# Attention stage of a two-layer transformer kernel: VectorE keeps the row-maximum stretch for itself, preparation of later batches moves ahead of it, residual add moves to GpSimd

## The chip, the cores and the metric

One NeuronCore of a Trainium2 chip runs the whole kernel. The metric is the device time of one execution in microseconds. The engines are TensorE (PE; its weight loads are listed as PEld), VectorE (DVE), ScalarE (ACT), GpSimd (POOL) and SyncE (SP, which issues transfers).

## The reference

The input `x` has 16 batches of 256 rows by 256 columns; `ctx` has the same shape. Layer 0 is a decayed sum over the rows and a feed-forward block with 4-bit weights. Layer 1 is the attention that this change is about, and then a feed-forward block with block floating point. Cut to the attention:

```python
q = layernorm(x); k = v = ctx                  # 16 heads of 16 columns each
q = q * cos + rotate_half(q) * sin             # k likewise
scores = einsum('bqhd,bkhd->bhqk', q, k) * hd ** -0.5 + slope[h] * (key - query)
attn = softmax(scores)
x = x + tanh(g_xattn[1]) * einsum('bhqk,bkhd->bqhd', attn, v)
```

## The kernel before

Every engine has its own written program, and semaphores tie them together. All 16 batches of `x` stay in SBUF (`xres`). After layer 0 the attention runs over batches 0 to 15, one body (`at_body`) each. Bodies 0, 1, 14 and 15 are written out, and 2 to 13 are a loop of two bodies a turn (`over_batches`).

A body for batch b overlaps three batches. On PE, it first turns (transposes) the operands of batch b+1: eight turns of `a_stack` into `a_ps_t` (`at_turn`, L561), which ACT casts into `stack_t` (L910). Between turns 1 and 2 it turns out the result of batch b-1 (`at_turn_out`, L623). This is called the first part here. In the second part PE makes, for batch b+1, sixteen pairs of matmuls for the row maxima (`at_scores_for_max`, L579, called M0 to M15) and mixes them with the sixteen pairs of the scores of batch b (`at_scores`, L600, S0 to S15) and eight groups of probabilities times values (`at_times_v`, L615, PV0 to PV7). DVE reduces every M to row maxima (`at_row_max`, L1497, R0 to R15). ACT takes the exponential of every S (`at_exponent`, L919, E0 to E15). M, S and their PSUM buffers alternate between the row halves 0 to 63 and 64 to 127 by the parity of their index, and each half has one buffer. So M(m) waits for R(m-2), S(u) waits for E(u-2), and PV(g) waits for E(2g+1). At the end of a body PE turns the maxima (`at_turn_max`, L586), which waits for R15.

The two parts of DVE's body carry, beside the maxima, the preparation of batch b+2: layernorm statistics (`at_qk_a`, L1451 to L1457), the normed q (`at_qk_norm`, L1463 and L1466), the rope sums (`at_rope`, L1475) and a cast of the rounded high half into the stack (`at_high_part`, L1487). They also carry the reciprocal and share of batch b-1 (L1504, L1508) and its gated residual add (L1511). POOL does the rope products (L1148, L1149, L1158, L1159), the reciprocal root (L1153) and the low half of the stack (`at_low_part`, L1141). Before, the k side and the norm stand in DVE's first part, and the rope sum and cast of q stand inside the sixteen maxima, at m = 5 and m = 8.

## Time and profile before

| | |
|---|---|
| median of 3 runs | 862.73 us (856.55 to 863.42) |
| the profiled execution | 860.34 us, span 858.2 us |
| busy share of the span | PE 83%, DVE 83%, ACT 57%, POOL 50% |
| attention bodies 0 to 15 | about 377 to 697 us of the span |
| mean granted PE clock | 0.93; 1.00 in the loop of the attention |

The page gives busy time, the chain of work that ended last and the costliest groups. The timeline gives single instructions, neighbours of one line merged into one row, and what ended the idle time before them.

### The profile page before, as it was taken

What the parts mean: (1) busy time and instruction counts of PE and PEld (TensorE: products, weight loads), DVE (VectorE), ACT (ScalarE), POOL (GpSimd) and SP (SyncE); (2) the same over time, 40 slices, a digit from 0 to 9 for tenths busy, and PEclk for the clock granted to TensorE, in tenths of its full rate; (3) what the DMA queues carried; (4) which work ended last, traced back from release to release, by engine and by line L of the source; (5) the groups of instructions that cost most, each with busy time, mean ns of one, the idle gap of its engine ahead of it and who ended that gap; (6) DMA issues with size and microseconds to landing.
All of it is one profiled execution on the core that took longest, in us unless ns stands there. A gap on an engine that the chain in (4) does not pass through costs nothing.

```text
span 858.2 us, 16571 instructions
## 1 busy us (share of the span) xinstructions
PE 713.5 (83%) x5090; PEld 517.0 (60%) x5090; DVE 708.5 (83%) x1230; ACT 488.0 (57%) x939; POOL 431.1 (50%) x331
## 2 busy tenths in 40 slices
PE   2255999999999998779999999999999775777775
PEld 1255888887888877556565555656565333444444
DVE  6867788998889887868898989898888658888885
ACT  3433545445454342337777777777778674555553
POOL 4524565555655545644444554555443526655553
PEclk8576999999999999879999999999999987888898
DMA  8800000000000000010000000000001000100011
GB/s 279 246 3 0 1 1 1 0 0 0 0 0 1 1 1 1 1 50 2 3 2 2 1 1 1 2 1 1 1 1 50 2 1 1 37 25 24 26 37 50
DMA packets 17719, 18.35 MB, mean 21 GB/s; under 512 B 1670, under 2 KB 16912, under 8 KB 17680
## 3 DMA queue, kind: packets, MB, share of 16 engines
q1 hardware_dynamic: 17084, 17.66, 6.4%
q8 instruction: 21, 0.34, 0.2%
q10 hardware_dynamic: 596, 0.20, 0.1%
q14 instruction: 18, 0.15, 0.1%
HBM read 13.39 MB, written 4.19 MB: 20 GB/s over the span
## 4 chain that ended last, share of the span: by engine, by line
PE 33%; DVE 30%; issue 16%; POOL 9%; ACT 8%; DVEq 1%; DMA 1%; POOLq 1%; ACTq 0%; SPq 0%
PE a_ps_t L561 7%; PE a_ps_m L579 6%; DVE maxima L1497 5%; PE a_ps_pv L615 4%; DVE f_ps_small L1582 4%; PE a_ps_s L600 3%; POOL hs L1110 3%; PE ps_o L522 3%; DVE hup L1324 2%; DVE f_hcode L1598 2%; DVE yup L1293 2%; POOL xres L1090 2%; DVE hscale L1318 2%; ACT hmag L866 1%; PE a_ps_pv L623 1%
## 5 line engine op out<-in xcount | busy, mean ns | idle before, releaser
L1497 DVE TENSOR_REDUCE maxima<-a_ps_m 128x2 f32<-128x512 f32 x256 | 166.3, 687 | 35.4 <-PE a_ps_m L579 34.7
L919 ACT ACTIVATE probs<-a_ps_s 128x512 f32<-128x512 f32 x256 | 149.2, 602 | 42.3 <-PE a_ps_s L600 40.1
L579 PE MATMUL a_ps_m<-stack_t 64*128 64x256 f32 x512 | 107.5, 328 | 19.9 <-DVE maxima L1497 16.7
L579 PEld LDWEIGHTS a_ps_m<-stack_t 64*128 64x128 f32 x512 | 68.3, 188 | 78.7 <-DVE maxima L1497 49.5
L600 PE MATMUL a_ps_s<-stack_t 64*128 64x256 f32 x512 | 100.0, 308 | 3.7 <-ACT probs L919 2.9
L1141 POOL TENSOR_TENSOR stack<-roped,stack 128x512 f32<-128x512 f32 x32 | 42.6, 1333 | 116.8 <-DVE stack L1487 115.3
L491 PE MATMUL ps_gu<-w1h,yth 128*128 128x352 f32 x256 | 88.6, 346 | 13.2 <-DVE h L1311 13.2
L522 PE MATMUL ps_o<-w2t,hqt 128*128 128x256 f32 (+1 forms) x384 | 97.9, 390 | 0.2 <-ACT hqt L851 0.2
L615 PE MATMUL a_ps_pv<-probs,v_aug 128*32 128x256 f32 x1024 | 83.0, 396 | 2.9 <-ACT probs L919 2.5
L910 ACT CAST stack_t<-a_ps_t 128x512 fp32r<-128x512 f32 x128 | 70.9, 588 | 24.5 <-PE a_ps_t L561 23.7
L561 PE MATMUL a_ps_t<-idf,stack 128*128 128x128 f32 x512 | 77.2, 294 | 9.0 <-POOL stack L1141 4.6
L492 PE MATMUL ps_gu<-w1l,yth 128*128 128x352 f32 x256 | 84.2, 329 | 0.0
L493 PE MATMUL ps_gu<-w1h,ytl 128*128 128x352 f32 x256 | 84.1, 328 | 0.0
L843 ACT ACTIVATE sg<-ps_gu 128x352 f32<-128x352 f32 x64 | 29.6, 462 | 84.3 <-PE ps_gu L493 84.3
L522 PEld LDWEIGHTS ps_o<-w2t,hqt 128*128 128x128 f32 (+1 forms) x384 | 66.4, 189 | 17.5 <-issue 10.6
L600 PEld LDWEIGHTS a_ps_s<-stack_t 64*128 64x128 f32 x512 | 68.5, 187 | 12.7 <-ACT probs L919 6.6
L561 PEld LDWEIGHTS a_ps_t<-idf,stack 128*128 128x128 f32 x512 | 58.8, 148 | 22.0 <-ACT stack_t L910 8.1
L1116 POOL TENSOR_TENSOR hq<-hcode,hscale 128x1408 f32<-128x1408 bf16 x16 | 41.4, 2590 | 49.5 <-DVE hcode L1330 49.5
L1190 POOL TENSOR_TENSOR f_hup<-f_h,f_hmag 128x2048 f32<-128x2048 f32 x16 | 58.2, 3640 | 10.5 <-DVE f_hcode L1598 9.5
L491 PEld LDWEIGHTS ps_gu<-w1h,yth 128*128 128x128 f32 x256 | 49.5, 193 | 18.6 <-DVE h L1311 17.5
L980 ACT ACTIVATE f_h<-f_ps_fc 128x512 f32<-128x512 f32 x64 | 36.1, 597 | 36.0 <-POOL f_hup L1190 33.7
L703 PE MATMUL f_ps_h<-idb,f_hcode 128*128 128x128 bf16 x256 | 25.9, 261 | 33.6 <-DVE f_hcode L1598 33.5
(176 smaller groups left out, 1613.3 us busy)
## 6 DMA issues: line engine op xcount, KB each, us to landing
xres<-in_x SPq DMA_DIRECT2D x16, 256.0 KB, 3.2
...
stack_t<-neg_max_t SPq DMA_DIRECT2D x32, 8.0 KB
```

The source lines that it names most:

```text
L491: nc.tensor.matmul(into, yth[:, kc, c, :], w1h[:, kc, cols], start=kc == 0, stop=False)
L492: nc.tensor.matmul(into, yth[:, kc, c, :], w1l[:, kc, cols], start=False, stop=False)
L493: ins = nc.tensor.matmul(into, ytl[:, kc, c, :], w1h[:, kc, cols], start=False, stop=kc == KD - 1)
L522: ins = nc.tensor.matmul(ps_o[:, c, :], hqt[0:rows, g, n, :], w2t[0:rows, k, :], start=k == 0, stop=k == KH0 - 1)
L561: ins = nc.tensor.transpose(a_ps_t[:, g % 2, (n * C + c) * P:(n * C + c + 1) * P], a_stack[:, b.par, which, c, 2 * pair:2 * pair + 2, :].r ...
L579: ins = nc.tensor.matmul(a_ps_m[:, half, n, :], a_stack_t[b.par][rows, 0, pair, c * P:(c + 1) * P], a_stack_t[b.par][rows, 1, pair, :], st ...
L600: ins = nc.tensor.matmul(a_ps_s[:, half, n, :], a_stack_t[b.par][rows, 1, pair, kc * P:(kc + 1) * P], a_stack_t[b.par][rows, 0, pair, :], ...
L615: ins = nc.tensor.matmul(a_ps_pv[32 * n:32 * n + 32, quad % 2, 0:T], a_v_aug[:, b.par, kc, 4 * quad + n, :], a_probs[:, (2 * g + n % 2) % ...
L910: nc.scalar.copy(a_stack_t[b.par][:, g % 2, pair:pair + 2, :].rearrange("p a t -> p (a t)"), a_ps_t[:, g % 2, :]).then_inc(a_t, 1)
L919: nc.scalar.activation(a_probs[:, u % 8], a_ps_s[:, u % 2], ACT.Exp).then_inc(a_exp, 1)
L1190: nc.gpsimd.tensor_tensor(f_blocks(f_hup[:, :]), f_blocks(f_h[:, b.par]), f_spread(f_hmag[:, b.par], F_NBH), ALU.add).then_inc(f_g_hup, 1)
L1497: nc.vector.tensor_reduce(a_maxima[:, b.par, c, 4 * quad + half:4 * quad + half + 3:2], a_ps_m[:, half], X, ALU.max).then_inc(a_v_max, 1)
```

## The change

PE issues S2 ahead of M0, and then S(m+3) right after M(m), where it was S(m+2) for m up to 6 and S(m+1) for m from 8 to 14. So the pair of matmuls behind an M uses the other row half. PV(m // 2) stands after every odd m. DVE keeps nothing but the sixteen maxima in the second part. The rope sum and cast of q join those of k in the first part, the statistics are those of batch b+4 and the norm that of batch b+3. The residual add leaves DVE: the gate is multiplied into the values on ACT, and POOL adds (`at_add`). The one semaphore chain of the preparation is split into seven. Ahead of the bodies DVE prepares batches 1 to 3 inside the maxima of batch 0. The feed-forward block's statistics wait for POOL's add. The diff, cut to its core, in the order of PE, ACT, GpSimd and VectorE:

```diff
@@ -635,20 +633,18 @@
                         at_turn_out(b.shifted(-1))
                     if nxt:
                         at_turn(nxt, g)
-                u = 0
                 for g in range(6, TG):
-                    at_scores(b, u)
+                    at_scores(b, g - 6)
                     if nxt:
                         at_turn(nxt, g)
-                    u += 1
+                at_scores(b, 2)
                 for m in range(MU):
                     if nxt:
                         at_scores_for_max(nxt, m)
-                    if m % 8 != 7:
-                        at_scores(b, u)
-                        u += 1
-                        if u % 2 == 0 and u >= 4:
-                            at_times_v(b, (u - 4) // 2)
+                    if m + 3 < SU:
+                        at_scores(b, m + 3)
+                    if m % 2 == 1:
+                        at_times_v(b, m // 2)
...
-                nc.scalar.copy(a_v_aug[:, b.par, :, :, 0:HD].rearrange("p c h d -> p (c h) d"),
-                               tiles(ctx, b).rearrange("p c (h d) -> p (c h) d", d=HD)).then_inc(a_v, 1)
+                nc.scalar.mul(a_v_aug[:, b.par, :, :, 0:HD].rearrange("p c h d -> p (c h) d"),
+                              tiles(ctx, b).rearrange("p c (h d) -> p (c h) d", d=HD), gates[:, 1:2]).then_inc(a_v, 1)
...
+                else:
+                    pool.wait_ge(a_v_rope, upto(V_ROPE, b.shifted(-1), "rope_k"))
...
+                pool.wait_ge(a_v_norm, upto(V_NORM, b, "norm1"))
+                if b.shifted(-1):
+                    pool.wait_ge(a_v_rope, upto(V_ROPE, b.shifted(-1), "rope_q"))
...
+            def at_add(b):
+                pool.wait_ge(a_v_out, upto(V_OUT, b, "share1"))
+                nc.gpsimd.tensor_tensor(tiles(xres, b), tiles(xres, b), a_attn[:, :, :], ALU.add).then_inc(a_g_add, 1)
 
             def at_body(b):
-                nxt2 = b.shifted(2)
+                nxt2, nxt3, nxt4 = b.shifted(2), b.shifted(3), b.shifted(4)
                 if nxt2:
-                    at_k_parts(nxt2)
-                    at_rstd(nxt2)
                     at_low_part(nxt2, 1)
-                    at_q_parts(nxt2)
                     at_low_part(nxt2, 0)
-                elif b.shifted(1):
+                if nxt3:
+                    at_q_parts(nxt3)
+                if b.shifted(-1):
+                    at_add(b.shifted(-1))
+                if nxt4:
+                    at_rstd(nxt4)
+                if nxt3:
+                    at_k_parts(nxt3)
+                if b.shifted(1) and not nxt2:
...
+            at_rstd(second)
             at_k_parts(second)
-            at_rstd(second)
+            at_q_parts(second)
             at_low_part(second, 1)
-            at_q_parts(second)
             at_low_part(second, 0)
-            over_batches(pool, at_body)
+            at_rstd(third)
+            at_k_parts(third)
+            at_q_parts(third)
+            at_rstd(fourth)
+            over_batches(pool, at_body, ATT_AHEAD)
...
+                if b.shifted(-1):
+                    dve.wait_ge(a_g_q, b.shifted(-1).count(2, 2))
...
+                dve.wait_ge((a_g_q, a_g_k)[which], b.count(2, 2))
+                if b.shifted(-1):
+                    dve.wait_ge(a_g_low, upto(G_LOW, b.shifted(-1), ("q_lo", "k_lo")[which]))
...
-            def at_add_attention(b):
+            def at_share(b):
...
+                if b.shifted(-1):
+                    dve.wait_ge(a_g_add, b.shifted(-1).count(1, 1))
...
-                dve.wait_ge(a_v_out, upto(V_OUT, b, "share1"))
-                nc.vector.scalar_tensor_tensor(tiles(xres, b).rearrange("p c d -> p (c d)"), a_attn[:, :, :].rearrange("p c d -> p (c d)"),
-                                               gates[:, 1:2], tiles(xres, b).rearrange("p c d -> p (c d)"),
-                                               ALU.mult, ALU.add).then_inc(a_v_out, 1)
 
             def at_body(b):
-                nxt2 = b.shifted(2)
+                nxt2, nxt3, nxt4 = b.shifted(2), b.shifted(3), b.shifted(4)
                 if nxt2:
-                    at_qk_a(nxt2)
                     at_rope(nxt2, 1)
                     at_high_part(nxt2, 1)
-                    at_qk_norm(nxt2)
-                if b.shifted(-1):
-                    at_add_attention(b.shifted(-1))
+                if b.shifted(-1):
+                    at_share(b.shifted(-1))
+                if nxt2:
+                    at_rope(nxt2, 0)
+                    at_high_part(nxt2, 0)
+                if nxt4:
+                    at_qk_a(nxt4)
+                if nxt3:
+                    at_qk_norm(nxt3)
                 if b.shifted(1) and not nxt2:
                     w34_magic(0)
                 for m in range(MU):
...
-                    if nxt2 and m == 5:
-                        at_rope(nxt2, 0)
-                    if nxt2 and m == 8:
-                        at_high_part(nxt2, 0)
...
+                dve.wait_ge(a_g_add, b.count(1, 1))
+                dve.sem_inc(f_alone, 1)
...
-            at_rope(second, 1)
-            at_high_part(second, 1)
             at_qk_norm(second)
             for m in range(MU):
                 at_row_max(first, m)
+                if m == 3:
+                    at_rope(second, 1)
+                    at_high_part(second, 1)
                 if m == 5:
                     l0_add_ffn(last)
                     at_rope(second, 0)
-                if m == 8:
                     at_high_part(second, 0)
-            over_batches(dve, at_body)
-
-            dve.wait_ge(a_g_qk, len(G_QK) * B)
+                if m == 9:
+                    at_qk_a(third)
+                if m == 12:
+                    at_qk_norm(third)
+                if m == 14:
+                    at_qk_a(fourth)
+            over_batches(dve, at_body, ATT_AHEAD)
```

On PE, body 0, from turn 6 on; `a_ps_m` takes an M, `a_ps_s` an S, `a_ps_pv` a PV. Before:

```order
L561 MATMUL a_ps_t<-idf,stack 128x128 x4
L600 MATMUL a_ps_s<-stack_t 128x256 x2
L561 MATMUL a_ps_t<-idf,stack 128x128 x4
L579 MATMUL a_ps_m<-stack_t 128x256 x2
L600 MATMUL a_ps_s<-stack_t 128x256 x2
L579 MATMUL a_ps_m<-stack_t 128x256 x2
L600 MATMUL a_ps_s<-stack_t 128x256 x2
L615 MATMUL a_ps_pv<-probs,v_aug 32x256 x4
L579 MATMUL a_ps_m<-stack_t 128x256 x2
L600 MATMUL a_ps_s<-stack_t 128x256 x2
L579 MATMUL a_ps_m<-stack_t 128x256 x2
```

And now:

```order
L559 MATMUL a_ps_t<-idf,stack 128x128 x4
L598 MATMUL a_ps_s<-stack_t 128x256 x2
L559 MATMUL a_ps_t<-idf,stack 128x128 x4
L598 MATMUL a_ps_s<-stack_t 128x256 x2
L577 MATMUL a_ps_m<-stack_t 128x256 x2
L598 MATMUL a_ps_s<-stack_t 128x256 x2
L577 MATMUL a_ps_m<-stack_t 128x256 x2
L598 MATMUL a_ps_s<-stack_t 128x256 x2
L613 MATMUL a_ps_pv<-probs,v_aug 32x256 x4
L577 MATMUL a_ps_m<-stack_t 128x256 x2
L598 MATMUL a_ps_s<-stack_t 128x256 x2
```

S2 moved ahead of M0, and S4 ahead of PV0.

On VectorE, body 1 from the norm (before) or the reciprocals (now) to its end. Before:

```order
L1466 TENSOR_SCALAR qn<-xres,a_mv,a_rstd 128x256 [waits v_qk]
L1466 TENSOR_SCALAR qn<-xres,a_mv,a_rstd 128x256
L1504 RECIPROCAL denom<-a_ps_pv 128x16 [waits a_t_out] x2
L1508 TENSOR_TENSOR attn<-a_ps_pv,denom 128x256 [waits a_v_out] x2
L1511 SCALAR_TENSOR_TENSOR xres<-attn,gates,xres 128x512 [waits a_v_out]
L1497 TENSOR_REDUCE maxima<-a_ps_m 128x2 [waits a_t_mt,a_t_m]
L1497 TENSOR_REDUCE maxima<-a_ps_m 128x2 [waits a_t_m] x5
L1475 TENSOR_TENSOR roped<-part_cos,part_sin 128x512 [waits g_qk]
L1497 TENSOR_REDUCE maxima<-a_ps_m 128x2 [waits a_t_m] x3
L1487 CAST stack<-roped 128x64x16 [waits a_t_t,v_qk]
L1497 TENSOR_REDUCE maxima<-a_ps_m 128x2 [waits a_t_m] x7
```

And now:

```order
L1519 RECIPROCAL denom<-a_ps_pv 128x16 [waits a_t_out] x2
L1525 TENSOR_TENSOR attn<-a_ps_pv,denom 128x256 [waits a_v_out] x2
L1490 TENSOR_TENSOR roped<-part_cos,part_sin 128x512 [waits a_g_low,a_g_q_parts]
L1502 CAST stack<-roped 128x64x16 [waits a_t_t,a_v_rope]
L1464 BN_STATS a_stats<-xres 128x6 x2
L1468 BN_AGGR a_mv<-a_stats 128x2 [waits a_v_stats] x2
L1470 TENSOR_SCALAR a_var<-a_mv 128x2 [waits a_v_stats]
L1475 TENSOR_SCALAR a_rstd<-a_rstd 128x2 [waits a_g_rstd]
L1480 TENSOR_SCALAR qn<-xres,a_mv,a_rstd 128x256 [waits a_g_q_parts,a_v_norm]
L1480 TENSOR_SCALAR qn<-xres,a_mv,a_rstd 128x256
L1512 TENSOR_REDUCE maxima<-a_ps_m 128x2 [waits a_t_mt,a_t_m]
L1512 TENSOR_REDUCE maxima<-a_ps_m 128x2 [waits a_t_m] x15
```

The maxima are one run of sixteen, and everything else stands ahead of them.

## Rows read from the trace of the kernel before

**Rows 1.** busy us (x instructions) of PE, PEld, DVE, ACT, POOL; PEclk, DMA share, GB/s
```profile
500.00:550.00 50.00, 46.42 (x438) 30.03 (x437) 43.75 (x85) 38.62 (x78) 21.85 (x17) 1.00 0.00 1
```

**Rows 2.** waits, 380 to 655 us: engine line <- releaser: us in total, times, longest
```profile
DVE maxima L1497 <- PE a_ps_m L579: 27.8, 43, 3.9
```

**Rows 3.** timeline of DVE, one body: start us, us, instructions, [idle before <-releaser]
```profile
515.70 0.74 DVE L1451 BATCH_NORM_STATS2 a_stats<-xres 128x6 f32 x2
...
516.90 0.69 DVE L1475 TENSOR_TENSOR roped<-part_cos,part_sin 128x512 f32<-128x512 f32 x1
...
520.45 0.76 DVE L1508 TENSOR_TENSOR attn<-a_ps_pv,denom 128x256 f32<-128x256 f32 x2
521.38 0.78 DVE L1511 SCALAR_TENSOR_TENSOR xres<-attn,gates,xres 128x512 f32 x1 [0.17 <-DVE attn L1508]
522.84 2.58 DVE L1497 TENSOR_REDUCE maxima<-a_ps_m 128x2 f32<-128x512 f32 x4 [0.69 <-PE a_ps_m L579]
525.96 1.29 DVE L1497 TENSOR_REDUCE maxima<-a_ps_m 128x2 f32<-128x512 f32 x2 [0.54 <-PE a_ps_m L579]
...
529.64 0.68 DVE L1487 CAST stack<-roped 128x1024 fp32r<-128x1024 f32 x1
530.24 2.57 DVE L1497 TENSOR_REDUCE maxima<-a_ps_m 128x2 f32<-128x512 f32 x4
533.12 1.98 DVE L1497 TENSOR_REDUCE maxima<-a_ps_m 128x2 f32<-128x512 f32 x3 [0.32 <-PE a_ps_m L579]
535.01 0.42 DVE L1451 BATCH_NORM_STATS2 a_stats<-xres 128x6 f32 x1
```

**Rows 4.** timeline of PE in the same body, turns of the stacks and first maxima
```profile
521.20 0.50 PE L600 MATMUL a_ps_s<-stack_t 64*128 64x256 f32 x2
...
522.22 0.52 PE L579 MATMUL a_ps_m<-stack_t 64*128 64x256 f32 x4
...
523.59 0.50 PE L579 MATMUL a_ps_m<-stack_t 64*128 64x256 f32 x2
523.93 0.40 PE L600 MATMUL a_ps_s<-stack_t 64*128 64x256 f32 x2
524.18 0.50 PE L579 MATMUL a_ps_m<-stack_t 64*128 64x256 f32 x2
...
524.85 0.64 PE L615 MATMUL a_ps_pv<-probs,v_aug 128*32 128x256 f32 x8
525.42 0.56 PE L579 MATMUL a_ps_m<-stack_t 64*128 64x256 f32 x4
```

**Rows 5.** timeline of PE in the same body, maxima 11 and 12
```profile
531.58 0.38 PE L579 MATMUL a_ps_m<-stack_t 64*128 64x256 f32 x1
531.59 0.38 PE L600 MATMUL a_ps_s<-stack_t 64*128 64x256 f32 x1
...
532.01 0.64 PE L615 MATMUL a_ps_pv<-probs,v_aug 128*32 128x256 f32 x8
532.58 0.38 PE L579 MATMUL a_ps_m<-stack_t 64*128 64x256 f32 x1
```

**Rows 6.** timeline of ACT in the same body, first exponentials
```profile
521.79 0.60 ACT L919 ACTIVATE probs<-a_ps_s 128x512 f32<-128x512 f32 x1
522.32 0.58 ACT L910 CAST stack_t<-a_ps_t 128x512 fp32r<-128x512 f32 x1
```

**Rows 7.** instructions on the tile qn: min/median/max ns, first and last start us
```profile
L1466 DVE TENSOR_SCALAR qn<-xres,a_mv,a_rstd x32: 401/412/1381, 335.0 to 637.1; 128x256 f32 x24, 128x256 f32<-128x256 f32 x8
```

**Rows 8.** timeline of PE, then DVE, body 14 (no batch left to prepare)
```profile
652.39 0.38 PE L586 MATMUL a_ps_m<-idf,maxima 128*16 128x128 f32 x2
...
654.88 0.69 DVE L1508 TENSOR_TENSOR attn<-a_ps_pv,denom 128x256 f32<-128x256 f32 x2
...
659.42 2.64 DVE L1497 TENSOR_REDUCE maxima<-a_ps_m 128x2 f32<-128x512 f32 x4 [0.41 <-PE a_ps_m L579]
```

**Rows 9.** timeline of DVE ahead of the bodies, last row maxima of batch 0
```profile
374.62 1.29 DVE L1497 TENSOR_REDUCE maxima<-a_ps_m 128x2 f32<-128x512 f32 x2 [0.35 <-PE a_ps_m L579]
```

More of the change, by code:

```diff
@@ L124 @@
 V_ROUND = ["up", "codes"]
-V_QK = ["stats0", "stats1", "aggr0", "aggr1", "var", "rope_k", "k_hi", "rstd4", "norm0", "norm1", "rope_q", "q_hi"]
-V_QK_FIRST = ["stats0", "stats1", "aggr0", "aggr1", "var", "rope_k", "rstd4", "norm0", "norm1", "k_hi", "rope_q", "q_hi"]
-G_QK = ["k_cos", "k_sin", "rstd", "k_lo", "q_cos", "q_sin", "q_lo"]
-G_QK_FIRST = ["k_cos", "k_sin", "rstd", "q_cos", "q_sin", "k_lo", "q_lo"]
-V_OUT = ["recip0", "recip1", "share0", "share1", "add"]
+V_STATS = ["stats0", "stats1", "aggr0", "aggr1", "var"]
+V_NORM = ["rstd4", "norm0", "norm1"]
+V_ROPE = ["rope_k", "k_hi", "rope_q", "q_hi"]
+G_LOW = ["k_lo", "q_lo"]
+V_OUT = ["recip0", "recip1", "share0", "share1"]
 V_IN1 = ["amax", "pow2", "magic"]
@@ L137 @@
 L0_BEHIND = 4
+ATT_AHEAD = 4
 FFN_AHEAD = 6
@@ L330, in build_main @@
         a_v_aug_laid = sem("v_aug_laid_out")
[L331 removed]
+        a_v_stats, a_v_norm, a_v_rope = sem("a_v_stats"), sem("a_v_norm"), sem("a_v_rope")
+        a_g_rstd, a_g_k, a_g_q, a_g_low = sem("a_g_rstd"), sem("a_g_k_parts"), sem("a_g_q_parts"), sem("a_g_low")
+        a_v_max, a_v_out = sem("v_max"), sem("a_v_out")
         a_t_t, a_t_m, a_t_s, a_t_pv, a_t_out, a_t_mt = (sem(f"a_{n}") for n in ("t_t", "t_m", "t_s", "t_pv", "t_out", "t_mt"))
@@ L1136, in at_low_part @@
             def at_low_part(b, which):
-                pool.wait_ge(a_v_qk, upto(v_qk_steps(b), b, ("q_hi", "k_hi")[which]))
+                pool.wait_ge(a_v_rope, upto(V_ROPE, b, ("q_hi", "k_hi")[which]))
                 lo = (HD, R_HI2)[which]
@@ L1239, in _ @@
             ff_input_up(lead[1])
+            at_add(last)
             ff_input_rstd(lead[4])
@@ L1691, in _ @@
             ff_input_shift(lead[3])
-            at_add_attention(last)
+            at_share(last)
             ff_input_magic(lead[2])
```

50 lines of the change are left out of this document (22 added, 28 removed).

## Prediction

> **What bounds the kernel now.** I read the busy time by stretch first. In the attention PE runs at its full granted clock and is busy for 46.4 of 50 us, DVE for 43.8 [rows 1]. Both look full, so neither share names the bound. The waits say more: DVE stands idle ahead of its row maxima for 27.8 us, 43 times, until PE delivers an M [rows 2]. So the maxima wait for PE, and PE in turn waits for DVE's release of a buffer. What counts is the loop between the two, which the timeline of one body shows.
>
> One body lasts from 515.70 to 535.01 on DVE, 19.31 us [rows 3]. Its first part goes to R0 at 522.84, with 0.69 us of idle time just ahead of it [rows 3]. Body 14, which prepares nothing, has R0 at 659.42, 7.03 us after the turn of the maxima at 652.39 [rows 8]. There DVE was free of all preparation and R0 came no earlier, so PE's turns set the length of the first part, not DVE.
>
> In the second part a maximum takes 0.69 us and ready ones follow at 0.61 (525.96 plus 1.29, less 0.68) [rows 3]. A row of four takes 2.58, and between the fours lie gaps: 0.54 ahead of R4 and 0.32 ahead of R13 [rows 3]. They come from PE's order. M3 waits for R1 and starts at 524.18, S5 stands behind it in the same row half, PV1 starts at 524.85, M4 at 525.42 and R4 at 525.96 [rows 3, 4]. That is 0.67, 0.57 and 0.54 us. DVE works off R2 and R3 in that time and runs dry. The rope sum and the cast fall into the same stretch. A cast costs 0.60 (529.64 to 530.24) [rows 3], but the maxima behind it then find their M ready, so part of the 0.60 was a gap that would be there anyway.
>
> **The change, step by step**, on this body, with the turn of the maxima at its place.
>
> 1. DVE's second part loses a rope sum and a cast, 0.60 each, 1.20 in all. If DVE were the bound this would be the gain. What it is really worth is whatever the gaps leave over, so I walk PE's order.
>
> 2. The opposite halves. Where an M waits for DVE, the S behind it in the other half starts with it: M11 at 531.58 and its S at 531.59, PV at 532.01, the next M at 532.58 [rows 5]. That is 0.43 to the PV, where the same half takes 0.67 [rows 4]. The change saves 0.24 in each four of the first half of the body. The second half has this order already. Its four costs 2.88 (530.24 to 533.12) [rows 3]. The Trainium skill (TensorEngine Tiling (Array Packing), Theoretical Speedup) gives up to 2x for a contraction of at most 64 rows. The rows here show 0.24 for a waiting pair. By the page alone every pair would gain, which is the ceiling behind the first rival.
>
> 3. S2 ahead of M0, S4 ahead of PV0. Now S2 starts at 522.22, where M0 was, and M0 follows in the same half 0.34 later, as S4 follows M2 (523.59, 523.93) [rows 4]. E2 can start 0.59 after S2, as E1 after S1 (521.20, 521.79), but ACT has the last cast at 522.32 and takes 0.51 for an instruction, so 522.83 [rows 4, 6]. It ends at 523.43. S4 waits for it and starts at 523.48, with the 0.05 that M2 shows after R0's end (522.84 plus 0.69, 523.59). Then PV0 0.43 later, 523.91, M2 at 524.48 and R2 at 525.02. Before, R2 came at 524.12. So this step loses 0.90 in the body's first four.
>
> 4. From R2 on the pattern of the second half repeats, with one gap in four: R14 three fours later, 525.02 plus 3 times 2.88, 533.66. R15 follows 0.61 later at 534.27 and DVE is free at 534.88, where it was at 535.01. Steps 1 to 4 together save 0.13 us a body. The 1.20 of DVE and the 0.24 of the halves are eaten by the 0.90 and by gaps that nothing fills any more.
>
> 5. DVE's first part gets fuller. Counted from the turn of the maxima, the share starts at 2.49 (652.39, 654.88) [rows 8] and takes 0.76 [rows 3]. Behind it now come the q rope sum 0.69 and 0.1 for its wait, the cast 0.60, the statistics 1.20 (515.70 to 516.90) [rows 3], and the norm: 0.2 for the small scale and two of 0.40. The norm took up to 1.38 where it ran beside POOL's low part, and 0.40 alone [rows 7]; now the statistics lie between the cast that starts the low part and the norm. Sum: 2.49 + 0.76 + 0.79 + 0.60 + 1.20 + 1.00 = 6.84, against R0 at 7.03 from PE. It is hidden with 0.2 us to spare, and more with S2's delay. If it were not, the excess would be paid in every body.
>
> 6. The add, 0.78 on DVE [rows 3], goes to POOL, and so do longer chains of waits. POOL was busy 21.9 of 50 us [rows 1] and its new order gives each product a whole body of lead. During the second part DVE reads its maxima from PSUM. Nothing for either side. Bounds: a loss of 0.2 or a gain of 0.2 a body. The gate on ACT is one scaled copy for a copy: nothing.
>
> 7. Ahead of the bodies DVE gets 2 statistics and a norm more inside batch 0's maxima, 2.4 + 1.0 = 3.4 us. Gaps of 0.35 in each pair there [rows 9] take up about 1.0, and the earlier norm of batch 1 lets the first maxima start about 1.0 sooner. Loss 1.4, bounds 0 and 3.4. Body 0 gives 0.5 back, since DVE has no share in it. Net loss 0.9.
>
> 8. The feed-forward block: each of 16 statistics gets one more wait and its own semaphore step. The nearest row is the 0.17 ahead of the add [rows 3]. Bounds 0 and 2.7 us; I take 0.8, because part of them fall beside idle time. In the tail PV7 stands ahead of the first feed-forward matmuls and DVE loses one add: gain 0.3.
>
> Sum: bodies 1 to 13, 13 times 0.13, -1.7; +0.9; +0.8; -0.3. Together -0.3 on the profiled 860.3 us, so 860.0. The median of the runs is 2.4 above the profiled one, so the same change on it gives **862.4 us**: no change that can be told.
>
> **The rivals.**
>
> *DVE was the bound* (chance 0.08). For it: 43.8 of 50 busy, and 1.20 us leaves the maxima. Then sixteen maxima take sixteen times 0.645, 10.3, from 522.84, and a body ends at 533.2 instead of 535.0, less the 0.3 by which R0 is later. That is 1.5 us, 13 times, 19.5: 843. Against it: the gap of 0.32 in the second half, where the halves are opposite already.
>
> *S4 does not hold PE* (0.14). If S2's exponential comes earlier, or PE takes PV0 and M2 past the waiting S4, only part of the 0.90 is lost. With two thirds of it back, 0.6 and 0.13 a body, 13 times, 9.5 us: 853. For it: PE's records show M0 and M1 as one row of four ahead of the S of the first half [rows 4], so something passes. Against it: each engine's waits are in order.
>
> *DVE's first part becomes the bound* (0.14). The place is between the share and R0. It decides when the norm meets POOL's q low part: the first norm then takes up to 1.38 for 0.40, 1.0 more, or waits on the new semaphores do the same. 6.84 becomes 7.8, 0.6 beyond S2-delayed R0 at 7.2, less 0.13: 0.5 a body, 13 times, 6.5 plus 1.4 of steps 7 and 8, about 8: 871. For it: the spare is only 0.2 to 0.4, and four new waits stand in that part. Against it: low part and norm are 1.2 us of statistics apart, and POOL's low part needs about that. The Trainium skill (GPSIMD Engine Reference, Specifications) says that GpSimd's SBUF interfaces are shared with VectorE instructions in a two-port mode or with two SBUF inputs; by that rule the cause of the long norm is the overlap, and the spread from 0.40 to 1.38 agrees.
>
> **How the numbers follow.** The forecast has 0.64, with its own range from 856 to 869: 0.3 us a body either way on the walk's 0.13, and the bounds of steps 6 to 8. The range over all cases is 850 to 870: it takes in most of the second rival and half of the last, and leaves out the first. About 1% is what a measurement of this kernel can tell from no change, 8.6 us. Below 854 lie the first rival, two thirds of the second and a little of the forecast: 0.18. Above 871 lies half of the last rival and a little more: 0.10. Within: 0.72.
>
> **What the profile after would show.** Right: R0 to R15 in rows of 2, 4, 4, 4 and 2, with an idle time of some 0.75 ahead of R2 and 0.3 to 0.4 ahead of R6, R10 and R14; S4 starting right at E2's end; a body of 19.2 us; R0 waiting for PE. Wrong in step 3: no long gap ahead of R2. Wrong in step 5: the norm ends right ahead of R0 with no idle time between, or takes over 0.5. Wrong in step 7: the turn of the maxima of batch 0 earlier than 377 or later than 380. What would make the sum wrong most easily is step 3, because 0.90 us hangs on one exponential.

## The result, and the profile after

The changed kernel takes 869.33 us in the median of 6 runs (866.68 to 870.02), against 862.01 us for the kernel before on the same chip (6 runs, 856.55 to 863.42). The ratio is 1.0092, with a 95% interval from 1.0062 to 1.0122: slower by 7.3 us. The time of 862.4 forecast is missed by 6.9 us, though the 869.33 lies just inside the range. "No change" was the wrong call. The profiled execution of the changed kernel has a span of 867.8 us, 9.6 more than the 858.2 of before.

The stages show where the 9.6 us lie. A body is counted here from one turn of the maxima to the next, and the last stage but one ends at the start of the last `pv_t` copy, read from the timelines of PE and ACT. All numbers are us, from one profiled execution of each kernel.

| stage | before | after | difference | forecast |
|---|---|---|---|---|
| start to the turn of the maxima of batch 0 | 377.01 | 379.63 | +2.62 | +1.4 |
| body 0 | 21.65 | 21.98 | +0.33 | -0.5 |
| bodies 1 to 13 | 253.74 | 252.35 | -1.39 | -1.7 |
| body 14 | 22.55 | 23.12 | +0.57 | 0 |
| last turn of the maxima to the last `pv_t` copy | 21.79 | 26.87 | +5.08 | -0.3 |
| from there to the end | 161.46 | 163.85 | +2.39 | +0.8 |

The loop of the attention, on which most of the working was spent, came out as forecast: its bodies take 19.15 and 19.70 us in turn, where they took 19.32 and 19.77. The loss stands at its two ends and in the feed-forward block.

First the busy time of 50 us of the loop, which answers to [rows 1] (PE, PEld, DVE, ACT, POOL; then PEclk, DMA share, GB/s), and the waits from 383 to 657 us, which answer to [rows 2]:

```profile
503.00:553.00 50.00, 47.34 (x446) 29.86 (x444) 41.31 (x84) 40.04 (x81) 27.13 (x23) 1.00 0.00 1
```

```profile
DVE maxima L1512 <- PE a_ps_m L577: 35.3, 71, 3.3
```

DVE is busy for 2.4 us less in 50 and waits for PE's maxima 71 times and not 43. The work that left DVE became waiting. The timeline of one body on DVE answers to [rows 3]:

```profile
521.90 0.69 DVE L1502 CAST stack<-roped 128x1024 fp32r<-128x1024 f32 x1
522.51 0.74 DVE L1464 BATCH_NORM_STATS2 a_stats<-xres 128x6 f32 x2
...
524.09 0.73 DVE L1480 TENSOR_SCALAR qn<-xres,a_mv,a_rstd 128x256 f32 x2
525.45 1.29 DVE L1512 TENSOR_REDUCE maxima<-a_ps_m 128x2 f32<-128x512 f32 x2 [0.63 <-PE a_ps_m L577]
527.36 2.64 DVE L1512 TENSOR_REDUCE maxima<-a_ps_m 128x2 f32<-128x512 f32 x4 [0.62 <-PE a_ps_m L577]
530.25 2.64 DVE L1512 TENSOR_REDUCE maxima<-a_ps_m 128x2 f32<-128x512 f32 x4 [0.24 <-PE a_ps_m L577]
533.13 2.64 DVE L1512 TENSOR_REDUCE maxima<-a_ps_m 128x2 f32<-128x512 f32 x4 [0.24 <-PE a_ps_m L577]
536.01 1.29 DVE L1512 TENSOR_REDUCE maxima<-a_ps_m 128x2 f32<-128x512 f32 x2 [0.24 <-PE a_ps_m L577]
537.22 0.68 DVE L1490 TENSOR_TENSOR roped<-part_cos,part_sin 128x512 f32<-128x512 f32 x1
```

The maxima come in rows of 2, 4, 4, 4 and 2, 2.89 and 2.88 us apart, with a long gap ahead of R2 and a short one ahead of R6, R10 and R14. The norm is done at 524.82 and DVE is idle for 0.63 ahead of R0. PE in the same body answers to [rows 4]:

```profile
524.58 0.61 PE L598 MATMUL a_ps_s<-stack_t 64*128 64x256 f32 x3
524.92 0.28 PE L577 MATMUL a_ps_m<-stack_t 64*128 64x256 f32 x1
...
525.83 0.50 PE L598 MATMUL a_ps_s<-stack_t 64*128 64x256 f32 x2 [0.28 <-ACT probs L914]
526.26 0.64 PE L613 MATMUL a_ps_pv<-probs,v_aug 128*32 128x256 f32 x8
526.83 0.38 PE L577 MATMUL a_ps_m<-stack_t 64*128 64x256 f32 x1
...
528.71 0.38 PE L577 MATMUL a_ps_m<-stack_t 64*128 64x256 f32 x1
...
529.14 0.64 PE L613 MATMUL a_ps_pv<-probs,v_aug 128*32 128x256 f32 x8
529.71 0.38 PE L577 MATMUL a_ps_m<-stack_t 64*128 64x256 f32 x1
```

S4 waits for E2 until 525.83, PV0 starts 0.43 later, M2 0.57 after that. The last three rows are M5, PV2 and M6. They show what sets the pace from R4 on. R3 ends at 528.65 and M5 starts 0.06 later, PV2 0.43 after M5, M6 0.57 after PV2, R6 0.54 after M6, and R6 and R7 take 1.29. That is 2.89 us, and then M9 waits for R7 as M5 waited for R3. No exponential ends a wait in it: S8, which goes out with M5, could have gone 0.2 us earlier.

### The profile page after: what moved, and what is told of

It reads as the page before. It is cut to its first block, busy times and chain, and to the rows that moved or that the text cites. A ratio compares the mean times of both kernels' runs of the same rounds, so it can differ in the third digit from the quotient of the medians.

```text
span 867.8 us, 16559 instructions
## 1 busy us (share of the span) xinstructions
PE 716.1 (83%) x5075; PEld 515.6 (59%) x5090; DVE 696.5 (80%) x1214; ACT 488.2 (56%) x939; POOL 435.3 (50%) x347
## 4 chain that ended last, share of the span: by engine, by line
PE 39%; DVE 25%; issue 15%; POOL 8%; ACT 8%; DMA 3%; DVEq 1%; POOLq 1%; SPq 1%; ACTq 0%
PE a_ps_m L577 9%; PE a_ps_pv L613 7%; PE a_ps_t L559 6%; DVE f_ps_small L1598 4%; PE a_ps_s L598 4%; POOL hs L1105 3%; PE ps_o L520 3%; DMA ctx<-in_ctx 2%; DVE maxima L1512 2%; DVE hup L1337 2%; DVE f_hcode L1614 2%; DVE yup L1306 2%; ACT probs L914 2%; DVE hscale L1331 2%; POOL xres L1085 2%
## 5 line engine op out<-in xcount | busy, mean ns | idle before, releaser
L914 ACT ACTIVATE probs<-a_ps_s 128x512 f32<-128x512 f32 x256 | 145.4, 598 | 20.0 <-PE a_ps_s L598 18.9
L598 PE MATMUL a_ps_s<-stack_t 64*128 64x256 f32 x512 | 117.4, 334 | 10.0 <-ACT probs L914 8.5
L577 PE MATMUL a_ps_m<-stack_t 64*128 64x256 f32 x512 | 110.1, 320 | 10.3 <-DVE maxima L1512 8.3
L577 PEld LDWEIGHTS a_ps_m<-stack_t 64*128 64x128 f32 x512 | 74.2, 188 | 67.3 <-DVE maxima L1512 42.6
L598 PEld LDWEIGHTS a_ps_s<-stack_t 64*128 64x128 f32 x512 | 75.4, 190 | 27.0 <-ACT probs L914 15.8
L613 PE MATMUL a_ps_pv<-probs,v_aug 128*32 128x256 f32 x1024 | 85.7, 408 | 0.2 <-ACT probs L914 0.2
L905 ACT CAST stack_t<-a_ps_t 128x512 fp32r<-128x512 f32 x128 | 70.9, 588 | 24.2 <-PE a_ps_t L559 23.4
L489 PEld LDWEIGHTS ps_gu<-w1h,yth 128*128 128x128 f32 x256 | 48.7, 190 | 19.9 <-DVE h L1324 18.8
```

The lines of the kernel that those rows point to most:

```text
L489: nc.tensor.matmul(into, yth[:, kc, c, :], w1h[:, kc, cols], start=kc == 0, stop=False)
L577: ins = nc.tensor.matmul(a_ps_m[:, half, n, :], a_stack_t[b.par][rows, 0, pair, c * P:(c + 1) * P], a_stack_t[b.par][rows, 1, pair, :], st ...
L598: ins = nc.tensor.matmul(a_ps_s[:, half, n, :], a_stack_t[b.par][rows, 1, pair, kc * P:(kc + 1) * P], a_stack_t[b.par][rows, 0, pair, :], ...
L613: ins = nc.tensor.matmul(a_ps_pv[32 * n:32 * n + 32, quad % 2, 0:T], a_v_aug[:, b.par, kc, 4 * quad + n, :], a_probs[:, (2 * g + n % 2) % ...
L905: nc.scalar.copy(a_stack_t[b.par][:, g % 2, pair:pair + 2, :].rearrange("p a t -> p (a t)"), a_ps_t[:, g % 2, :]).then_inc(a_t, 1)
L914: nc.scalar.activation(a_probs[:, u % 8], a_ps_s[:, u % 2], ACT.Exp).then_inc(a_exp, 1)
```

## The experiments

The theories were these. **A**: PE's new order eats what DVE gives, in the loop and in the last body. **B**: the order makes no difference, other waits moved. **C**: the last body lost its time to a lower granted clock. (In the expectations of e1 and e2, C stands for another rival: the last body alone is at fault.) Head and feed-forward block have questions of their own.

### The order of PE taken back, and the order alone

`e1_old_pe_order` is the changed kernel with this edit, `e2_new_pe_order_alone` the kernel before with its reverse:

```diff
-                at_scores(b, 2)
                 for m in range(MU):
                     if nxt:
                         at_scores_for_max(nxt, m)
-                    if m + 3 < SU:
-                        at_scores(b, m + 3)
-                    if m % 2 == 1:
-                        at_times_v(b, m // 2)
+                    if m % 8 != 7:
+                        at_scores(b, u)
+                        u += 1
+                        if u % 2 == 0 and u >= 4:
+                            at_times_v(b, (u - 4) // 2)
...
+                at_times_v(b, PG - 1)
                 if nxt:
                     at_turn_max(nxt)
```

> The changed kernel with PE's whole order of before (S2 behind M0, S(m+2) up to m 6, S(m+1) from m 8, PV7 last); DVE, POOL and ACT as changed. Theory A, PE's new order eats what DVE gives: the idle time of 1.3 from R1 to R2 shrinks to about the 0.68 of before, 13 bodies from 252.3 us (19.4 each) to 243 to 247 (18.7 to 19.0), and the last body from 26.9 us to about 22: 853 to 858 in all. Rival B, the order of PE makes no difference and only other waits moved: bodies stay at 252 us, 866 to 869. Rival C, only the last body is at fault: bodies 252, last body 22, 864.

> The kernel before with nothing but PE's new order. Theory A: R2 comes 0.9 later in each body, the rope sum and the cast stay in the maxima's stretch, so 13 bodies take 253.7 plus 4 to 10 us, and the last body 5 us more: 870 to 877. Rival B: bodies at 253 to 254 us, last body as before: 862. Rival C: bodies 253 to 254, last body 27: 867.

Measured: e1 856.24 us in the median of 10 runs, ratio to before 0.9944 (0.9924 to 0.9964). e2 874.74 us, ratio 1.0174 (1.0141 to 1.0206), both beside a kernel before of 860.73. The stages, with two kernels of further below:

| stage | before | after | e1 | e2 | e9 | e11 |
|---|---|---|---|---|---|---|
| to the turn of batch 0 | 377.0 | 379.6 | 379.6 | 376.1 | 379.3 | 376.9 |
| body 0 | 21.7 | 22.0 | 21.3 | 23.1 | 21.8 | 21.2 |
| bodies 1 to 13 | 253.7 | 252.4 | 245.9 | 258.8 | 252.3 | 245.9 |
| last turn to last `pv_t` copy | 21.8 | 26.9 | 23.4 | 27.3 | 25.6 | 22.5 |
| from there to the end | 161.5 | 163.9 | 161.8 | 162.9 | 161.8 | 158.1 |

Theory A holds. B falls, and so does C of these two expectations, since the bodies of the loop moved with the order. The order costs 6.5 us in bodies 1 to 13 of the changed kernel (245.9 to 252.4) and 5.1 us in those of before (253.7 to 258.8). All the rest of the change gives 7.8 us there (253.7 to 245.9), which is 0.60 a body, half of the 1.20 that left the maxima. One body of e1 on DVE, then of e2, then the middle of e1's body on PE:

```profile
521.63 2.57 DVE L1515 TENSOR_REDUCE maxima<-a_ps_m 128x2 f32<-128x512 f32 x4 [0.39 <-PE a_ps_m L577]
524.75 3.26 DVE L1515 TENSOR_REDUCE maxima<-a_ps_m 128x2 f32<-128x512 f32 x5 [0.54 <-PE a_ps_m L577]
528.31 2.57 DVE L1515 TENSOR_REDUCE maxima<-a_ps_m 128x2 f32<-128x512 f32 x4 [0.31 <-PE a_ps_m L577]
531.31 1.97 DVE L1515 TENSOR_REDUCE maxima<-a_ps_m 128x2 f32<-128x512 f32 x3 [0.42 <-PE a_ps_m L577]
```

```profile
526.08 1.29 DVE L1494 TENSOR_REDUCE maxima<-a_ps_m 128x2 f32<-128x512 f32 x2 [0.92 <-PE a_ps_m L579]
528.00 2.64 DVE L1494 TENSOR_REDUCE maxima<-a_ps_m 128x2 f32<-128x512 f32 x4 [0.63 <-PE a_ps_m L579]
```

```profile
524.20 0.55 PE L577 MATMUL a_ps_m<-stack_t 64*128 64x256 f32 x4
524.55 0.44 PE L598 MATMUL a_ps_s<-stack_t 64*128 64x256 f32 x4
524.92 0.64 PE L613 MATMUL a_ps_pv<-probs,v_aug 128*32 128x256 f32 x8
...
526.78 0.38 PE L577 MATMUL a_ps_m<-stack_t 64*128 64x256 f32 x1 [0.19 <-DVE maxima L1515]
```

e1 has no gap ahead of R2 and one of 0.54 ahead of R4. With the new order the gap of 0.63 ahead of R2 is there in e2 too, with all of the DVE code of before. The first three rows of PE show four pairs in the old order: M4 and M5 are one row of four from 524.20, ahead of S6 that stands between them in the program, and PV2 starts after 0.72 us. M5, which waits for R3, starts at 524.25, so its PV follows after 0.67, where the changed kernel needs 0.43. The opposite halves do give the forecast 0.24 there. But the last row is M8 of e1: with no S and no PV between M7 and M8, it starts as soon as R6 has left its buffer, and R8 follows R7 without a gap. That is how five maxima come to stand in a row, and the new order has no such place. From R0 to R15 e1 takes 10.96 us, the changed kernel 11.17. R0 itself comes 7.01 us after the turn of the maxima in e1 and 7.25 in the changed kernel, where S2 stands ahead of M0. These two, 0.21 and 0.24, are the order's cost in this body.

### PV0 ahead of S4

```diff
+                    if m == 1:
+                        at_times_v(b, 0)
                     if m + 3 < SU:
                         at_scores(b, m + 3)
-                    if m % 2 == 1:
+                    if m % 2 == 1 and m > 1:
                         at_times_v(b, m // 2)
```

> The changed kernel; PE issues PV0 ahead of S4 and not behind it, in every body. Theory A, step 3 of the prediction: S4 waits for E2 and holds PV0 and M2 behind it. PV0 (0.57 us from its start to M2's) is then done in that wait, M2 starts 0.34 behind S4 and not 0.9 to 1.0, and the time from R1 to R2 falls from 1.33 to 0.7 to 0.9 us; the 13 bodies take 246 to 249 us, not 252.3: 863 to 866. Rival: something else holds M2 (its own wait for R0, or the mere position of S2 ahead of M0), R1 to R2 stays at 1.3: 869.

Measured: 871.10 us, ratio 1.0111 (1.0076 to 1.0146), and 252.19 us for bodies 1 to 13. The four maxima from R0 and the next rows:

```profile
525.73 2.67 DVE L1514 TENSOR_REDUCE maxima<-a_ps_m 128x2 f32<-128x512 f32 x4 [0.63 <-PE a_ps_m L577]
529.22 2.57 DVE L1514 TENSOR_REDUCE maxima<-a_ps_m 128x2 f32<-128x512 f32 x4 [0.82 <-PE a_ps_m L577]
```

R1 to R2 fell from 1.31 to 0.77 as theory A said, and the gain was given back whole two maxima later, in a gap of 0.82 ahead of R4. So theory A was right about the place and wrong about the worth: the body stayed as long, where 246 to 249 us were expected. In this body S4 starts 0.59 us after R0, E4 0.71 after S4, and S6, which waits for it, 0.65 after E4. This round trip of 1.36 us for two S is longer than the 1.29 that two maxima take, and PV1 and M4 stand behind S6. So at the start of the maxima the exponentials hold PE, at S4 in the changed kernel and at S6 here. From R4 on both kernels have the same pace, R4, R8 and R12 2.88 to 2.89 us apart. In the changed kernel that is the loop of M, PV, M and two maxima shown above, in which no S waits for its exponential; in e5 only S12 still does.

### S two behind M throughout

Would the old order gain if its S stayed at two ahead to the end? `e12_lag_two_throughout` is e11 (below) with one edit:

```diff
-                    if m % 8 != 7:
+                    if m < 14 if nxt else m % 8 != 7:
                         at_scores(b, u)
```

> The kernel of e11_best_of_both; PE issues S(m+2) behind M(m) up to m 13 in all bodies but the last, where it was S(m+1) from m 8. Theory: from R4 to R8 the maxima come at VectorE's own pace of 0.64 us with S(m+2), and from R8 on one in four comes 0.4 late with S(m+1); with S(m+2) throughout, R0 to R15 takes 10.3 to 10.6 and not 11.0, 13 bodies 239 to 242 us and not 245.9: 844 to 848. Rival, the exponentials can't follow (an S waits for the E two before it, 1.36 us a pair at best) and the gaps only come at other places: 245 to 247 us, 850 to 852.

Measured: 859.78 us, ratio 0.9993 (0.9979 to 1.0007), where e11 has 849.02. Bodies 1 to 13 take 254.7 us and not 245.9. My expectation of 844 to 848 was wrong, and so was the size of the rival's, 850 to 852: the loss is 9 us beyond it. The maxima fall into pairs from R8 on.

```profile
526.47 2.57 DVE L1515 TENSOR_REDUCE maxima<-a_ps_m 128x2 f32<-128x512 f32 x4 [0.55 <-PE a_ps_m L577]
529.66 1.29 DVE L1515 TENSOR_REDUCE maxima<-a_ps_m 128x2 f32<-128x512 f32 x2 [0.61 <-PE a_ps_m L577]
531.28 1.29 DVE L1515 TENSOR_REDUCE maxima<-a_ps_m 128x2 f32<-128x512 f32 x2 [0.34 <-PE a_ps_m L577]
```

The rival's cause is there, in part: S11 starts 0.05 us after E9's end, and PV4 and M10 stand behind it. But the largest gap, 0.61 ahead of R8, has another. With S9 and PV3 now between M7 and M8, M8 starts 1.30 us after M7, where e11 has 0.68. The edit moves the S and the PV from m = 7 on together, so what each is worth stays open. The two together are worth 0.68 us a body.

### The add back on VectorE

`e7_old_pe_order_add_on_vectore` is e1 with the add behind the shares on DVE:

```diff
+                dve.wait_ge(a_v_out, upto(V_OUT, b, "share1"))
+                nc.vector.tensor_tensor(tiles(xres, b), tiles(xres, b), a_attn[:, :, :], ALU.add).then_inc(a_g_add, 1)
...
-                if b.shifted(-1):
-                    at_add(b.shifted(-1))
```

> The kernel of e1_old_pe_order; the residual add goes back from POOL to VectorE, behind the shares. Theory (steps 5 and 6): VectorE's first part has 0.39 us to spare ahead of R0 in that kernel. The add takes 0.6 to 0.7, so R0 comes 0.2 to 0.3 later in each of 13 bodies: 245.9 becomes 248.5 to 250, and 859 to 861 in all. Rival, the spare is larger than the timeline tells, or PE is late with M0 too: 246 us, 856. Rival, the add on POOL slows what it runs beside, and taking it away gives more back: under 245 us, 854.

Measured: 862.44 us, ratio 1.0021 (1.0004 to 1.0037). Bodies 1 to 13 take 251.4 us, 5.6 more than in e1, 0.43 a body where I expected 0.2 to 0.3.

```profile
524.45 0.74 DVE L1480 TENSOR_SCALAR qn<-xres,a_mv,a_rstd 128x256 f32 x2
525.10 2.57 DVE L1512 TENSOR_REDUCE maxima<-a_ps_m 128x2 f32<-128x512 f32 x4
```

R0 follows the norm with no idle time. DVE's first part is the bound in this kernel, and only the add on POOL keeps it from being one. So the 0.60 a body of e1 needs both: the rope sum and the cast moved out of the maxima, and the add moved away to make room for them. The order of PE and the add on DVE each undo the whole gain: 856 us in e1, 862 with the add on DVE, 869 with the new order.

### The last body

Four kernels are the changed one with an edit in body 15 only. e3 puts the turns of the feed-forward weights ahead of S10, e6 adds 28 transposes that nobody reads, e10 does both with fewer transposes, e9 puts back PE's order of before:

```diff
+                    if not nxt and m == 7:
+                        turn_w34(2)
+                        turn_w34(3)
                     if m + 3 < SU:
                         at_scores(b, m + 3)
...
-                    if not nxt and m == 8:
-                        turn_w34(2)
-                        turn_w34(3)
```

```diff
+                def filler(n):
+                    for _ in range(n):
+                        nc.tensor.transpose(a_ps_t[:, 1, 0:P], idf[:, :], idf[:, :])
...
+                if not nxt:
+                    pe.wait_ge(a_t, TG * B)
+                    filler(12)
...
+                    elif m < 12:
+                        filler(1)
```

> The changed kernel; only in the last body the two turns of the second weight of the feed-forward block stand ahead of S10 and not behind S11. Theory: ACT's copies of them wait for turns that wait for S11, which waits for E9. Then ACT's idle time of 3.1 us ahead of the first w_proj_t copy shrinks to about 0.5, and the last body goes from 26.9 to 22 to 24 us: 865 to 867. Rival, the lower granted clock (0.66 there, 0.93 before) is the cause by itself: the last body stays above 26 us, 869.

> The changed kernel; in the last body alone PE also makes 28 transposes whose result nobody reads: 16 where it waits for the row maxima of batch 15, and one in the place of each of M0 to M11. Theory C, the lower granted clock (0.50 from 687 to 702 us, where before it was 0.66 to 1.00) comes of PE's idle time and makes much of the 5.1 us that the last body lost: the clock stays at 0.9 to 1.0 and the body takes 22.5 to 24.5 us and not 26.9: 866. Rival, the order of the waits alone is the cause: the body stays at 26 to 28 us, whatever the clock: 869 to 870.

> The changed kernel; PE's order of before in the last body alone (body 15; S2 keeps its new place there). Theory: what the last body and the start of the feed-forward block lost is all of PE's order: 26.9 us becomes 21 to 23.5 (by the clock it is granted there: the same order took 21.2 to 23.4 in the kernels run so far), and the first gelu of batch 1 follows the first of batch 0 after 6.7 us and not 8.0. Bodies 1 to 13 stay at 252.3: 862 to 865 in all. Rival, the last body is long because the loop ahead of it leaves a low clock: over 25 us, 868.

> The changed kernel with both edits of e3 and e6, the weight turns ahead of S10 and the unread transposes, with only 5 of these ahead of S2 so that they don't delay it. Theory: the order costs some 2 us and the lower clock some 1.5, each alone: from the first exponential of the last body to its last pv_t copy it took 22.1 us in the changed kernel, 20.1 with the turns earlier, 20.7 with the filler, 17.8 before. Both together give 18.5 to 19.5: 865 to 867. Rival, the two edits remove the same wait: 20 us or more, 868.

| kernel | median us | ratio to before (interval) | first exponential of body 15 to last `pv_t` copy |
|---|---|---|---|
| after | 869.3 | 1.0092 (1.0062 to 1.0122) | 22.1 |
| e3 | 868.4 | 1.0089 (1.0058 to 1.0120) | 20.1 |
| e6 | 869.4 | 1.0104 (1.0074 to 1.0133) | 20.7 |
| e9 | 863.8 | 1.0043 (1.0021 to 1.0066) | 20.6 |
| e10 | 863.3 | 1.0025 (1.0002 to 1.0047) | 26.2 |

e9 settles the sum: the old order in this body alone gives 4 to 6 us back, as its theory said. Where its profiled execution (866.2 us) gained them is less clear. The last stage but one took 25.6 us and not the expected 21 to 23.5, at a mean granted clock of 0.67 from the first exponential on. The start of the feed-forward block gave 1.34 back: from the first gelu of batch 0 to that of batch 1 it takes 4.80 us in the changed kernel, 4.4 to 5.3 in every kernel with the new order in this body, and 3.46 in each of the seven without. Of the other expectations, that of e3 (865 to 867) and that of e10 (865 to 867) were missed on either side, and e6 came out as its rival said: 26.97 us, 869.4. Rows of ACT in the changed kernel, then in e9:

```profile
689.70 1.07 ACT L914 ACTIVATE probs<-a_ps_s 128x512 f32<-128x512 f32 x2
693.86 1.93 ACT L798 COPY w_proj_t<-a_ps_m 128x1024 bf16<-128x1024 bf16 x2 [3.09 <-PE a_ps_m L448]
```

```profile
689.65 1.08 ACT L921 ACTIVATE probs<-a_ps_s 128x512 f32<-128x512 f32 x2
691.62 1.93 ACT L805 COPY w_proj_t<-a_ps_m 128x1024 bf16<-128x1024 bf16 x2 [0.89 <-PE a_ps_m L448]
```

In the changed kernel S10, PV3 and S11 stand ahead of the weight turns. S10 starts when E8 ends, at 690.34, the turns at 692.79, all at a granted clock of 0.50. ACT's copies stand right behind E9, which is done at 690.77: ACT idles for 3.09 us, and S12 in turn waits 1.66 us for ACT. In e9, with S9 and PV3 there, it is 0.89. e3 cut the 3.09 to 0.17 and the stretch from 22.1 to 20.1 us, both at a like granted clock (0.58 and 0.56 in the mean), yet its median fell by 1 us at most. Another part is the clock. Its windows of 5 us in e1 and e8 below (the same order of PE in this body), busy us of PE, PEld, DVE, ACT, POOL, then PEclk:

```profile
674.40:679.40 5.00, 5.00 (x36) 2.17 (x34) 3.45 (x15) 4.05 (x9) 1.56 (x4) 0.53 0.01 3
679.40:684.40 5.00, 5.00 (x44) 3.15 (x38) 2.95 (x10) 4.08 (x8) 1.93 (x3) 0.50 0.01 2
```

```profile
674.40:679.40 5.00, 3.43 (x30) 1.69 (x28) 3.64 (x17) 4.34 (x8) 2.63 (x3) 1.00 0.02 5
679.40:684.40 5.00, 4.80 (x52) 2.85 (x52) 3.17 (x11) 4.89 (x11) 1.71 (x2) 1.00 0.01 2
```

With the same instructions of PE and ACT in the same order this stretch, from the first exponential to the last `pv_t` copy, took 19.4 us in e1, where the clock was 0.50 for 10 us and 0.65 in the mean, and 17.2 in e8, with 0.90 in the mean. So the clock is worth about 2.2 us there. The changed kernel had 0.50 from 687 to 702 us. e6, whose clock was 1.00 from 687 to 697 and 0.86 in the mean, still took 20.7. Near the full clock the new order therefore costs about 3 us here (20.7 against 17.2 and 17.8, some of it the unread transposes), and the low clock the rest.

All profiled executions together say the same. With the old order in body 15 the stretch took 17.2 and 17.8 us at a mean granted clock of 0.90 (e8, before), 18.5 to 18.8 at 0.72 and 0.73 (e7, e11, e12), and 19.4 and 20.6 at 0.65 and 0.67 (e1, e9). With the new order and no other edit of this body it took 22.1 to 22.6 at 0.50 to 0.58 (after, e2, e4, e5). None of the old ones had so low a clock and none of these four a higher one. Whether the order itself brings the low clock is not taken apart. The unread transposes do not secure the clock: in the profiled execution of e10 PE was busy without a pause from 682 to 702 us at 0.50 for most of it, and the transposes then only lengthened the body.

```profile
687.00:692.00 5.00, 5.00 (x23) 2.62 (x27) 2.05 (x8) 2.70 (x6) 1.71 (x2) 0.50 0.00 0
692.00:697.00 5.00, 5.00 (x34) 3.26 (x38) 2.45 (x9) 3.13 (x5) 1.73 (x2) 0.50 0.01 2
```

That execution took 872 us, while the median of e10 is 863.3, so its profile does not speak for its runs. How e10's 6 us divide between wait and clock stays open, and so does why PE was granted the lower clock in some executions and not in others.

### The head

```diff
+                if m == 4:
+                    at_qk_a(third)
                 if m == 5:
+                    at_qk_a(fourth)
                     l0_add_ffn(last)
...
-                if m == 9:
-                    at_qk_a(third)
...
-                if m == 14:
-                    at_qk_a(fourth)
```

> The changed kernel; only ahead of the bodies the statistics of batches 2 and 3 stand behind R4 and R5 of batch 0, where DVE was idle for 0.6 and 1.2 us, and not behind R9 and R14. Theory: the turn of the maxima of batch 0 moves from 379.6 back to 377.3 to 378.3, so 1.3 to 2.3 us less: 867. Rival, PE is what is waited for in that stretch and a statistic costs wherever it stands: 379.5 again, 869.

Measured: 867.08 us, ratio 1.0067 (1.0043 to 1.0092), 2.2 less than the changed kernel, with intervals that overlap (1.0062 to 1.0122 there). The profile is clearer. The turn of the maxima of batch 0 came at 376.97, 2.7 us earlier and as early as before the change. DVE in the changed kernel, then a row of POOL there, then DVE in e4:

```profile
362.94 0.69 DVE L1512 TENSOR_REDUCE maxima<-a_ps_m 128x2 f32<-128x512 f32 x1 [0.58 <-PE a_ps_m L577]
364.86 0.69 DVE L1512 TENSOR_REDUCE maxima<-a_ps_m 128x2 f32<-128x512 f32 x1 [1.23 <-PE a_ps_m L577]
...
374.50 1.11 DVE L1475 TENSOR_SCALAR a_rstd<-a_rstd 128x2 f32<-128x2 f32 x1
375.65 0.73 DVE L1480 TENSOR_SCALAR qn<-xres,a_mv,a_rstd 128x256 f32<-128x256 f32 x2
```

```profile
374.33 1.27 POOL L1146 TENSOR_TENSOR part_sin<-ctx,sin 128x512 f32<-128x512 f32 x1
```

```profile
363.42 0.74 DVE L1464 BATCH_NORM_STATS2 a_stats<-xres 128x6 f32<-128x256 f32 x2
...
364.74 0.69 DVE L1512 TENSOR_REDUCE maxima<-a_ps_m 128x2 f32<-128x512 f32 x1
...
373.74 0.16 DVE L1475 TENSOR_SCALAR a_rstd<-a_rstd 128x2 f32<-128x2 f32 x1
```

The statistics fill the 1.23 us in which DVE waited for PE, and the small scale takes 0.16 and not 1.11. In the changed kernel it runs beside POOL's product, which starts before it and ends at 375.60, and the scale ends at 375.61. In e4 POOL has nothing to do from 373.1 to 374.75, when the scale runs.

### The waits of the feed-forward block

`e8_old_pe_order_one_wait` is e1 with two waits in place of sixteen:

```diff
 def ff_input_stats(b):
-                dve.wait_ge(a_g_add, b.count(1, 1))
-                dve.sem_inc(f_alone, 1)
...
+            dve.wait_ge(a_g_add, FFN_AHEAD)
             ff_input_stats(lead[0])
...
+            dve.wait_ge(a_g_add, B)
             over_batches(dve, ff_body, FFN_AHEAD, FFN_BEHIND)
```

> The kernel of e1_old_pe_order; the 16 waits and semaphore steps ahead of the statistics of the feed-forward block become two waits, one ahead of the first statistics and one ahead of the loop. Theory (step 8): they cost 0.10 to 0.16 us for each batch, so the block from the last gelu of batch 0 to the end is 1 to 2 us shorter: 854.5 to 855.5. Rival, they fell beside idle time of VectorE, which waits for the gelus there (0.2 to 0.7 us ahead of each maximum of the hidden rows): the block is as long as before the edit, 856.

Measured: 853.09 us, ratio 0.9903 (0.9878 to 0.9928), 3.1 less than e1. From the first gelu of batch 1 to the end it takes 154.1 us, 156.7 in e1. DVE ahead of a statistics, in e1 and in e8:

```profile
766.85 0.23 DVE L1608 TENSOR_SCALAR f_hmag<-f_ps_small 128x64 f32<-128x64 f32 x1
767.22 0.75 DVE L1558 BATCH_NORM_STATS2 f_stats<-xres 128x6 f32 x2
```

```profile
746.40 0.23 DVE L1606 TENSOR_SCALAR f_hmag<-f_ps_small 128x64 f32<-128x64 f32 x1
746.58 0.75 DVE L1556 BATCH_NORM_STATS2 f_stats<-xres 128x6 f32 x2
```

From the start of the small instruction to that of the statistics it is 0.37 us against 0.18: a wait that is long satisfied, with its semaphore step, costs DVE 0.19 us here. This place is inside the loop of the block, where the trace of e1 has a register instruction of 0.09 us and a semaphore instruction of 0.02 us more. All eight batches of the loop cost 0.18 to 0.20 each. The eight that are written out cost 0.06 or less. Together that is 1.8 us, inside the 1 to 2 of the theory, and it comes off the time, so the rival falls. What more the times of e1 and e8 differ by is not located. The seven kernels that share the instructions of this block with the changed one took 155.2 to 158.6 us for the same stretch, itself among them.

These waits are only part of this stage. e1 has them and takes just 0.3 us more than the kernel before, 161.8 and 161.5. Part of what it saves is the add on DVE for the last batch: the first gelu of batch 2 follows that of batch 1 after 11.1 us in e1, 11.9 in e7 with the add back on DVE, and 12.0 before.

### A version that beats both

`e11_best_of_both` is e8 with the edit of e4.

> VectorE, POOL and ACT as changed, PE's order of before, the statistics of batches 2 and 3 in the gaps of batch 0's maxima (e4), two waits for sixteen ahead of the feed-forward statistics (e8). Theory: the gains add: 853.1 of e8 less the 2.3 to 2.7 of e4: 850 to 851. Rival, the earlier turn of the maxima is given back in body 0: 853.

Measured: 849.02 us in the median of 5 runs, ratio 0.9873 (0.9850 to 0.9897): 12.2 us faster than the kernel before and 19 to 20 faster than the changed one. Expected were 850 to 851, so the gains add and nothing is given back in body 0 (21.2 us).

## Why the prediction was right or wrong

- **Steps 1, 3 and 4, the walk of the loop: right.** 13 bodies gained 1.39 us, forecast 1.7. A body takes 19.15 us, forecast 19.2 (every other one 19.70, as it took 19.77 before). R2 came 9.16 us after the turn of the maxima (518.20 to 527.36), where [rows 3] have 8.3 to 8.4. S4 starts 0.05 after E2's end. The fours repeat at 2.88 and 2.89, and the loop that makes them is the one that step 4 took over from the second half of the body. The gap ahead of R2 is 0.62 us for 0.75, the others 0.24 for 0.3 to 0.4.
- **Step 3, what the wait costs: only at its place.** e5 took PV0 out of the wait, and S6 waited for E4 instead. The body stayed as long.
- **Step 2, opposite halves: right in size, wrong in worth.** PV2 comes 0.43 us after M5, where e1 with the old halves has 0.67. But I compared with the kernel before, rope sum and cast included, and never walked the old order without them. That walk is e1, with five maxima in a row, and it is 0.50 us a body faster than the new order.
- **Step 5: right.** R0 waits for PE with 0.63 us to spare, the norm takes 0.37 each, and the rival of the long norm did not come.
- **Step 6: right that the add costs nothing on POOL, but its worth was not priced.** My own sum of 6.84 us of 7.03 shows it: 0.6 more would not have fitted. e7 measures it as 5.6 us.
- **Step 7, the head: mis-sized.** +2.62 and +0.33 us for a net 0.9. I let the gaps of the last maxima absorb 1.0 us. The added work stands where DVE had no gap, while the large gaps at 362 to 366 us stayed empty (e4), and the earlier start of R0 (358.41 for 359.40) was lost in them. 0.9 us of it is the small scale beside POOL's product.
- **Step 8, the tail: the step that failed.** I saw only that "PV7 stands ahead of the first feed-forward matmuls" and gave the tail a gain of 0.3 us. It lost 5.1 and, in the start of the feed-forward block, 1.34 more (4.80 us from the first gelu of batch 0 to that of batch 1, 3.46 before and in e1 and e9). I never walked PE's new order through body 15, where S10, PV3 and S11 now stand between E9 and the weight turns that ACT waits for, and I took the granted clock there as given: 0.90 in the mean from the first exponential to the last `pv_t` copy before, 0.58 after. e9 shows that the order in this one body is worth 4 to 6 us of the 7.3. How much of that is waiting and how much is the clock stays open.
- **Step 8, the waits: mis-sized.** 0.8 us taken. They cost 1.8 at their own places, and the medians of e1 and e8 differ by 3.1. The upper bound of 2.7 took the 0.17 of [rows 3] for all sixteen, and only the eight in the loop cost that much.
- **The sum and the range.** In every stage the measured time lies above the forecast, so no error hid another. The range is given as 850 to 870, but the chances beside it are counted for 854 and 871, so the 0.72 belongs to a range that starts at 854. All that the last paragraph of the prediction calls right did come. None of these signs looks at the last body or the feed-forward block.
- **The rivals.** None of the three was the case. The slower side was there, but by an unnamed mechanism, the last body. "DVE was the bound" held for neither kernel, though without the new order, and with the add on POOL, half of the 1.20 us does come through.
